# Four stages of attention and convolution on one core: a lap later for the values, a ring of three, scaled unit matrices for the inverses, ones in the first laps

## The reference

```python
x = _L0_conv_ref(x, ...)   # non-local block: theta, phi, g (64 channels), phi and g pooled 2x2 to M0 = 256
                           # softmax over the 256 pooled pixels, product with g, W, batch norm, + x
x = _L1_conv_ref(x, ...)   # wavelet block
x = _L2_conv_ref(x, ...)   # one head:  alpha = softmax(q^T k), out = v alpha^T, projection, + x
x = _L3_conv_ref(x, ...)   # eight heads of 16 channels: attn = softmax(q^T k * temp), out = v attn^T
                           # projection, + x, group norm, MLP, + x
```

## Time and profile before

| | |
|---|---|
| median of three runs | 1834.67 us (1830.48 to 1840.71) |
| the profiled execution | 1839.56 us, span 1838.0 us, mean granted TensorE clock 0.874 |
| PE | 1558.0 us busy (85%) |
| DVE | 1125.7 us (61%) |
| ACT | 816.3 us (44%) |
| POOL | 274.4 us (15%) |

### The profile page before, as it was taken

The page is one execution under the profiler, slowest core; times in us unless marked ns, Lnnn a source line. Parts: engine busy times, 40 slices in busy tenths (PEclk is TensorE's granted clock), DMA queues, the critical chain, the costliest instruction groups (busy, mean ns, idle before and its releaser), DMA issues.

```text
span 1838.0 us, 20837 instructions
## 1 busy us (share of the span) xinstructions
PE 1558.0 (85%) x6468; PEld 690.1 (38%) x6468; DVE 1125.7 (61%) x1912; ACT 816.3 (44%) x1514; POOL 274.4 (15%) x305
## 2 busy tenths in 40 slices
PE   6579769998889889899889898899889888986992
PEld 3236325433343335333353334333343335322430
DVE  5454564766568584877558574777567573766601
ACT  1113301465327552465327552466326562763770
POOL 5003012110130103110130102200140104010000
PEclk6779957998889899898889898998888899987995
DMA  2000022012120303011120303002020303022101
GB/s 51 12 12 7 6 35 47 12 20 50 22 45 7 81 1 64 8 29 53 19 49 7 81 1 59 14 18 64 12 54 7 69 3 64 7 69 43 29 12 36
DMA packets 31569, 58.64 MB, mean 32 GB/s; under 512 B 14678, under 2 KB 16862, under 8 KB 31456
## 3 DMA queue, kind: packets, MB, share of 16 engines
q1 hardware_dynamic: 27296, 50.41, 12.8%
q0 software_dynamic: 4160, 6.83, 2.5%
HBM read 14.37 MB, written 4.50 MB: 10 GB/s over the span
## 4 chain that ended last, share of the span: by engine, by line
PE 64%; DVE 15%; issue 9%; ACT 4%; DMA 3%; SPq 3%; POOL 2%; DVEq 0%; ACTq 0%; POOLq 0%
PE ps L1337 64%; DVE mx L1283 5%; DVE x L1189 3%; ACT p L1015 2%; DVE x L1232 1%; SPq L689 1%; DMA invw<-inverse_sums 1%; DMA qp<-q3h 1%; POOL kp L838 1%; DVE mx L1279 1%; DVE x L1237 1%; DVE x L1196 1%; DVE hn L1226 1%; DVE x L1195 1%; SPq L666 1%
## 5 line engine op out<-in xcount | busy, mean ns | idle before, releaser
L1283 DVE TENSOR_REDUCE mx<-ps 128x1 f32<-128x512 f32 x1024 | 647.9, 683 | 267.5 <-PE ps L1337 265.6
L1015 ACT ACTIVATE p<-ps 128x512 f32<-128x512 f32 x1024 | 551.4, 599 | 313.7 <-PE ps L1337 312.6
L1337 PE MATMUL ps<-kp,qp 63*128 63x512 f32 x1024 | 417.1, 508 | 69.7 <-DVE mx L1283 34.1
L1337 PE MATMUL ps<-qp,kp 64*128 64x512 f32 x1024 | 382.1, 468 | 17.1 <-ACT p L1015 12.4
L1337 PEld LDWEIGHTS ps<-qp,kp 64*128 64x128 f32 x1024 | 165.6, 192 | 359.0 <-ACT p L1015 283.4
L1337 PE MATMUL ps<-p,vt 128*32 128x512 f32 x2048 | 295.6, 633 | 3.8 <-ACT p L1015 2.4
L1337 PEld LDWEIGHTS ps<-kp,qp 63*128 63x128 f32 x1024 | 176.1, 203 | 192.6 <-DVE mx L1283 124.0
L980 ACT ACTIVATE p<-ps 128x512 f32<-128x512 f32 x128 | 76.3, 597 | 255.8 <-PE ps L1337 231.1
L1337 PE MATMUL ps<-p,vT 128*128 128x512 f32 x256 | 143.5, 662 | 2.5 <-ACT p L980 2.4
L849 POOL TENSOR_TENSOR acc<-acc,p 128x512 f32<-128x512 f32 x96 | 126.2, 1315 | 63.4 <-ACT p L980 60.3
L1279 DVE TENSOR_REDUCE mx<-ps 128x1 f32<-128x512 f32 x128 | 82.1, 682 | 37.2 <-PE ps L1337 37.2
(11 more groups left out here) (192 smaller groups left out, 1663.5 us busy)
## 6 DMA issues: line engine op xcount, KB each, us to landing
qp<-q3h SPq DMA_DIRECT2D x128, 64.0 KB, 2.9
xin<-in_x SPq DMA_DIRECT2D x8, 512.0 KB, 4.6
acc<-inverse_sums SPq DMA_DIRECT2D x16, 256.0 KB, 3.4
kp<-k3h POOLq DMA_DIRECT2D x64, 64.0 KB, 4.1
qp<-q3l SPq DMA_DIRECT2D x64, 64.0 KB, 3.2
x3a<-x SPq DMA_DIRECT2D x8, 512.0 KB, 4.6
kp<-k3h SPq DMA_DIRECT2D x64, 64.0 KB, 2.5
x3b<-x3a SPq DMA_DIRECT2D x8, 512.0 KB, 2.9
```

Source lines behind the costliest of these rows:

```text
L1015: a.activation(p3[:, s % 2, i, :], ps[:, SB + (u + 1) % 3, :], ACT.Exp).then_inc(sem("p3_ready"), 1)
L1283: v.tensor_reduce(mx3[:, i, c, h:h + 1], ps[:, bank, :], AX.X, ALU.max).then_inc(sem("mx3_ready"), 1)
L1337: return nc.tensor.matmul(o, l, r, start=start, stop=stop)
```

## The change

Four things are changed together.

1. The values product of the eight-head attention moves from the third to the fourth lap of the next step (`i == 3`). `p3` becomes a ring of three steps, taken by `step % RING` over both groups; the wait before a step's exponentials is for the values product of three steps before. The buffer `p2` of the one-head attention is now the third slot of that ring, so the first exponential of the one-head attention waits for the values product that read this slot last, and the third step's exponentials wait for all values and sums of the one-head attention.
2. The inverses of the first block. Eight products take 128 pixels of `x1` each as the weights and 64 columns of ones, so that the sums of 128 pixels lie on 128 partitions; DVE takes one reciprocal of 128x8 into `inv0`, and multiplies the unit matrix `ident` with four columns of it at a time, which makes four diagonal blocks in a half of `x1`; PE multiplies ones with that half, which puts the inverse of each pixel on all partitions, and ACT copies it to `x1`. The steps behind are numbered two higher.
3. `fill` in the first window puts four `keep_clock` products behind each of laps 0 to 17, where two stood in all.
4. The semaphores `v_ones` and `k_ones` become one, `heads_set`, and those who asked for either ask for all five writes.

Cut to its core (the tables of `STEADY` and `LAST` change in the same way as `FIRST`: products in steps 27, 29, 31, 33 and 35, ACT's copies in 30 and 32; in `STEADY` 29 and 31 are both in lap 155):

```diff
+RING = 3
-    "fill": "000000000110000000000000000000000000000000000000010000...
+    "fill": "444444444444444444000000000000000000000000000000010000...
-            "L0": {...27: 152, 29: 155, 31: 156, 33: 161},
+            "L0": {...27: 152, 29: 155, 31: 155, 33: 156, 35: 161},
...
-        p2 = sb("p2", [128, 4, HALF])
-        p3 = sb("p3", [128, 2, GH, HALF])
+        p3 = sb("p3", [128, RING, GH, HALF])
+        p2 = p3[:, RING - 1, :, :]
...
+                for h in range(NH):
+                    yield at(bt, "L0", 30 + 2 * h)
+                    wait(act, sem("inv0_ps"), bt, NH + 1, h + 2)
+                    a.copy(half(x1, h), ps[:, bank_of(bt), :]).then_inc(sem("inv0_ready"), 1)
...
+                elif u == 0:
+                    wait(act, sem("pv3_done"), bt + -2, NG * STEPS, NG * STEPS - 2)
...
-                            if i == 0 and step >= 2:
-                                wait(act, sem("pv3_done"), bt, NG * STEPS, step - 1)
+                            if i == 0 and step >= RING:
+                                wait(act, sem("pv3_done"), bt, NG * STEPS, step - RING + 1)
+                            elif i == 0 and step == RING - 1 and attention:
+                                wait(act, sem("pv2_done"), bt + 1, A2_TILES)
+                                wait(act, sem("acc_steps"), bt + 1, (NC - 1) * NH)
...
-                            a.activation(p3[:, s % 2, i, :], ps[:, SB + (u + 1) % 3, :], ACT.Exp).then_inc(sem("p3_ready"), 1)
+                            a.activation(p3[:, step % RING, i, :], ps[:, SB + (u + 1) % 3, :], ACT.Exp).then_inc(sem("p3_ready"), 1)
...
-                for h in range(NH):
-                    yield at(bt, "L0", 28 + 2 * h)
-                    wait(dve, sem("den0_ps"), bt, NH, h + 1)
-                    v.reciprocal(half(x1, h), ps[:, bank_of(bt), :]).then_inc(sem("inv0_ready"), 1)
+                yield at(bt, "L0", 28)
+                wait(dve, sem("inv0_ps"), bt, NH + 1, 1)
+                link(v.reciprocal(inv0[:], ps[:, bank_of(bt), 0::CI]))
+                for h in range(NH):
+                    v.tensor_tensor(half(x1, h).rearrange("p (c q) -> p c q", q=128), ident[:].unsqueeze(1).to_broadcast([128, NC // 2, 128]),
+                                    inv0[:, NC // 2 * h:NC // 2 * (h + 1)].unsqueeze(2).to_broadcast([128, NC // 2, 128]), ALU.mult).then_inc(sem("diag0_ready"), 1)
...
+                yield at(bt, "L0", 27)
+                wait(pe, sem("p0_added"), bt)
+                for c in range(NC):
+                    last = mm(ps[:, bank_of(bt), CI * c:CI * (c + 1)], part(x1, c), ones[:, 0:CI])
+                last.then_inc(sem("inv0_ps"), 1)
+                for h in range(NH):
+                    yield at(bt, "L0", 29 + 2 * h)
+                    wait(pe, sem("diag0_ready"), bt, NH, h + 1)
                     if h:
                         wait(pe, sem("inv0_ready"), bt, NH, h)
-                    else:
-                        wait(pe, sem("p0_added"), bt)
-                    mm(ps[:, bank_of(bt), :], ones[:], half(x1, h)).then_inc(sem("den0_ps"), 1)
+                    mm(ps[:, bank_of(bt), :], ones[:], half(x1, h)).then_inc(sem("inv0_ps"), 1)
...
-                        if heads and 0 <= q < HEAD_LAPS and i == 2 and s:
+                        if heads and 0 <= q < HEAD_LAPS and i == 3 and s:
...
-                                last = mm(ps[32 * k:32 * (k + 1), VB, :], vt3[g][:, j, k, :], p3[:, (s - 1) % 2, k, :],
+                                last = mm(ps[32 * k:32 * (k + 1), VB, :], vt3[g][:, j, k, :], p3[:, (g * STEPS + s - 1) % RING, k, :],
```

More of the change, by code:

```diff
@@ L520, in build @@
         x1 = sb("x1", [128, N])
+        inv0 = sb("inv0", [128, NC])
         fused = sb("fused", [128, Q])
@@ L706, in passes @@
                             if mb.is_number(0):
-                                sp.wait_ge(sem("k_ones"), 3)
+                                sp.wait_ge(sem("heads_set"), 5)
                             sp.dma_start(raw(nmrow[0:1, :]).rearrange("p (a b) -> p a b", b=128), raw(nm2T[:])).then_inc(sem("nm2_row_in"), 16)
@@ L834, in pack @@
                     if bt.is_number(0):
-                        pool_e.wait_ge(sem("k_ones"), 3)
+                        pool_e.wait_ge(sem("heads_set"), 5)
                     carry_wait(bt, g)
@@ L1007, in passes @@
                             step = g * STEPS + s
-                            if i == 0 and step >= 2:
-                                wait(act, sem("pv3_done"), bt, NG * STEPS, step - 1)
+                            if i == 0 and step >= RING:
[3 more added lines that the diff above has]
+                                wait(act, sem("acc_steps"), bt + 1, (NC - 1) * NH)
                             elif i == 0:
-                                wait(act, sem("pv3_done"), bt + -1, NG * STEPS, NG * STEPS - 1 + step)
+                                wait(act, sem("pv3_done"), bt + -1, NG * STEPS, min(NG * STEPS, NG * STEPS - 1 + step))
                             u = g * TILES + q
                             wait(act, sem("s3_ps"), bt, NG * TILES, u + 1)
-                            a.activation(p3[:, s % 2, i, :], ps[:, SB + (u + 1) % 3, :], ACT.Exp).then_inc(sem("p3_ready"), 1)
+                            a.activation(p3[:, step % RING, i, :], ps[:, SB + (u + 1) % 3, :], ACT.Exp).then_inc(sem("p3_ready"), 1)
                         if i == 3 and s and s % NC == 0:
@@ L1106, in late_start @@
                 for t in vt3:
-                    v.memset(t[:], 1.0).then_inc(sem("v_ones"), 1)
-                v.memset(raw(qp[:]), 0.0).then_inc(sem("k_ones"), 1)
-                v.memset(raw(nmrow[:]), 0.0).then_inc(sem("k_ones"), 1)
-                v.memset(raw(kp[:]), 1.0).then_inc(sem("k_ones"), 1)
+                    v.memset(t[:], 1.0).then_inc(sem("heads_set"), 1)
+                v.memset(raw(qp[:]), 0.0).then_inc(sem("heads_set"), 1)
+                v.memset(raw(nmrow[:]), 0.0).then_inc(sem("heads_set"), 1)
+                v.memset(raw(kp[:]), 1.0).then_inc(sem("heads_set"), 1)
             def linker(stage, bt, per):
@@ L1167, in non_local @@
             def non_local(bt):
-                link = linker("l0", bt, 2)
+                link = linker("l0", bt, 3)
                 for h in range(NH):
@@ L1185, in non_local @@
                                     ALU.max, negate=True).then_inc(sem("nm0_ready"), 1)
+                yield at(bt, "L0", 28)
+                wait(dve, sem("inv0_ps"), bt, NH + 1, 1)
+                link(v.reciprocal(inv0[:], ps[:, bank_of(bt), 0::CI]))
                 for h in range(NH):
[L1187 to L1189 removed]
+                    v.tensor_tensor(half(x1, h).rearrange("p (c q) -> p c q", q=128), ident[:].unsqueeze(1).to_broadcast([128, NC // 2, 128]),
+                                    inv0[:, NC // 2 * h:NC // 2 * (h + 1)].unsqueeze(2).to_broadcast([128, NC // 2, 128]), ALU.mult).then_inc(sem("diag0_ready"), 1)
                 for h in range(NH):
[L1191 removed]
+                    yield at(bt, "L0", 34 + 2 * h)
                     wait(dve, sem("y0_ps"), bt, NH, h + 1)
@@ L1442, in non_local @@
                     mm(ps[:, bank_of(bt), :], part(ph, k // NH), half(th, k % NH)).then_inc(sem("s0_ps"), 1)
+                yield at(bt, "L0", 27)
[3 more added lines that the diff above has]
+                last.then_inc(sem("inv0_ps"), 1)
                 for h in range(NH):
-                    yield at(bt, "L0", 27 + 2 * h)
+                    yield at(bt, "L0", 29 + 2 * h)
+                    wait(pe, sem("diag0_ready"), bt, NH, h + 1)
                     if h:
                         wait(pe, sem("inv0_ready"), bt, NH, h)
-                    else:
-                        wait(pe, sem("p0_added"), bt)
-                    mm(ps[:, bank_of(bt), :], ones[:], half(x1, h)).then_inc(sem("den0_ps"), 1)
+                    mm(ps[:, bank_of(bt), :], ones[:], half(x1, h)).then_inc(sem("inv0_ps"), 1)
                 for h in range(NH):
-                    yield at(bt, "L0", 31 + 2 * h)
+                    yield at(bt, "L0", 33 + 2 * h)
                     if h:
@@ L1610, in passes @@
                 if bt.is_number(0):
-                    pe.wait_ge(sem("v_ones"), 2)
+                    pe.wait_ge(sem("heads_set"), 5)
                     pe.wait_ge(sem("wo_in"), 16)
-                    pe.wait_ge(sem("k_ones"), 3)
+                    pe.wait_ge(sem("heads_set"), 5)
                 heads, attention = bt.exists(), (bt + 1).exists()
```

1 line of the change is left out of this document (removed), and 32 rows, old and new, of tables (FIRST, LAST, STEADY).

## The result

The changed kernel takes 1850.16 us (median of 19 runs, 1841.84 to 1866.84) against 1836.56 us (19 runs, 1829.01 to 1847.69) before: a ratio of 1.0076, 95% interval 1.0052 to 1.0100. It is slower by 14 us, where 40 us less were forecast.

A forecast was written before the change was run, and what follows sets the result against it. PE, 85% busy, idled 39.0 us for the first layer's reciprocal and 14.8 us for exponentials. Saving 26 + 8 + 2.5 + 3 = 39.5 us takes the profiled 1839.56 us to 1800 us, as a median 1795 us, range 1779 to 1817 us.

The forecast's parts named there:

- Values one lap later: Main loop: values product in the fourth lap cuts PE's waits for exponentials; 3 us less, between 14.8 gain and 9.4 loss.
- Denominators, five windows: Ends of windows 0 to 4: small products and a 128x8 reciprocal save 5.2 us each at full clock, 26 us.
- second and third image: First window: shorter waits for these images' last reciprocals and shorter pairs with `wg`; 2.5 us less, at most 5.9.
- the first rival: New denominator chains: the clock falls all the same, so only 16 us are gained, 1819 us; chance 0.12.
- First image: Start of first window: fillers keep the clock up and the new denominators are shorter; 8 us less (6 to 10).
- the fourth: Rival for the whole kernel: PE is the bound, so added fillers and small products cost their length, 1880 us; chance 0.03.
- The third: Rival at window ends: next window's maxima wait for DMA-brought `qp` rows, five windows gain nothing, 1827 us; chance 0.04.
- The sum: Whole kernel: 26 + 8 + 2.5 + 3 = 39.5 us less, forecast 1795 us; chance 0.76.

The follow-up runs named there:

- run 2: Kernel before with the values part alone: values product in the fourth lap, ring of three shared with p2; ratio to before 1.0216.
- run 9: Changed kernel with norm steps one lap later and the next image's first maxima tile moved from lap 92 to 93 in steady windows; 1805.11 us.
- run 1: Changed kernel with the values product back in the third lap, all else kept; 1802.36 us, ratio to before 0.9824.
- run 4: Changed kernel with the norm steps ahead of the eight heads one lap later in the steady windows; 1841.80 us, ratio to before 1.0033.
- run 5: Kernel before with the denominators part alone (small products, 128x8 reciprocal, scaled unit matrices, ACT's copies, joined semaphore); ratio to before 0.9873.
- run 7: Kernel before with denominators part and fillers, values product in the third lap, ring of two; ratio to before 0.9867.
- run 8: run 1's kernel with more first-window fillers: two behind each of laps 18 to 56, one behind each of laps 161 to 220; 1847.83 us.
- run 10: run 1's kernel with two fillers behind each of laps 18 to 56; 1804.66 us, ratio to before 0.9830.
- run 12: run 1's kernel with laps 92 to 95 holding 0, 0, 3, 2 maxima tiles in place of 1, 0, 3, 1; 1809.86 us.
- run 6: Kernel before with the fillers alone, four behind each of the first 18 laps; ratio to before 0.9993, 1.3 us less.

## Why the prediction was wrong

- **Values one lap later, -3 us (14.8 us of gain to 9.4 us of loss): this step failed.** Measured alone it is +40 us (32 to 47 by run 2's interval). Its first half came true and was worth little: in the trace of before the values product starts within 0.15 us of its fourth exponential in 63 of 256 steps, afterwards in 2; the third lap's score tile then starts so in 62, as was said. What the step left out was the other side of the move. I asked who waits for the values product and for how long, and priced that; I did not ask what the product had been lying beside. It stood in PE's order ahead of one more score tile and one more maxima tile, and the second of these waits for DVE or for a DMA at two places of every window. The Trainium skill (PSUM — Partial Sum Buffer, "Engine vs sequencer instructions") says that matmuls start in program order; the rows agree, since the product whose operands were there (the fourth exponential ended at 612.93 us) stands behind the tile that waits until 619.83 us. Two moves of steps, with the product left in the fourth lap, took back 45 of the 48 us (1850.2 to 1805.1 us), and PE's waits at the two places went with them, so these two places are shown to carry most of the loss. One reservation: neither move was run as it stands with the product in the third lap, and they may gain something by themselves (the second groups of run 9 are 5.7 us shorter than run 1's). The first groups keep 10.0 us of the loss in the table (412.6 against 402.6 us), 1.0 to 1.5 us in each window, which no run took apart.
- **Denominators, five windows, -26 us: held in mechanism and nearly in size; second and third image, -2.5 us: not shown.** Alone they gave 23 us (13 to 33) for the 28.5 us. By the traces the five ends gave 18.0 us in the changed kernel and 27.1 us in run 1. Images two and three gained nothing in the changed kernel: from the first product of the denominators to the end of the pair with `wg` they take 15.29 and 14.58 us, where they took 14.52 and 12.69 us, and the granted clock there is 0.67 and 0.53, where it was 0.76 and 0.73. At the windows' ends eight small products took 2.00 us at full clock (2.3 us by the row). The estimate from the formula of the Trainium skill (TensorE: Matmul & The Clock Gate, "LDWEIGHTS (loading the stationary operand)") was 1.7 us. DVE's part was covered by the values product and the maxima, as worked out. What kept the changed kernel at 18.0 us was the first rival, the low clock: it came in three windows of five there and in one of five in run 1. I had given it 0.12 for all five together. I had taken full clock because the longest idle stretch would be 0.65 us and 0.69 us had gone with the full rate; the stretches came out at 0.68 to 0.77 us, and the clock behind them was at either level. The move of the values product seems to have a part in it: with the new denominators the ends of windows 0 to 4 ran long in 3, 3 and 4 of five windows where the product stands in the fourth lap (the changed kernel, runs 4 and 9), and in 1, 1, 2, 0, 0 and 0 where it stands in the third (runs 1, 5, 7, 8, 10 and 12). How it would do so is open.
- **First image, -8 us: nearly right in the trace, not seen in the medians.** In the trace the pair starts 5.2 us earlier (forecast 6.3) and ends 6.8 us earlier (forecast 7.8). The stretch behind POOL's sum ran at the lower clock, as I had said of its start, but I had priced the small products at 2.3 us even there (3.67 us) and the pair was right (1.92 us). In the medians the fillers give 1.3 us (between 6.6 less and 4.0 more), while the trace of run 6 has a lead of 5.7 us up to the first pair of window 0. Whether it is lost later or only lies within the measurement is open.
- **The rivals.** The time came out on the side of the fourth, slower, to which I gave 0.03, but not by its mechanism: PE's busy time rose by 29.6 us, and run 6 shows that the fillers cost nothing. The third, that the next window doesn't follow because of rows of `qp` that DMAs bring, named the right wait in the wrong place: it is in the middle of the window, at the first maxima tile.
- **The sum.** With the values step at nothing the working gives 1798 us, and run 1, which leaves it out, has 1802 us. That they lie so near is in part luck: in the traces of run 1 and of before the window ends gave 27.1 us for the 26, the first window gave 2.9 us for the 10.5 of the three images, and the groups of four heads, for which this sum has nothing, gave 4.4 + 6.0 us.

## What to carry to other kernels

When a piece of work moves along an engine's order, price it twice: what it waits for in its new place, and what waits it was covering in the old one. To find the second, look in the trace for the stretches in which the other engines or DMAs are busy with something that this engine will need next, and see whether the moved piece runs there. A change of several parts is worth splitting before it is judged: here a gain of 23 us and a loss of 40 us stood in one edit.

## What was not expected of the hardware

- A short wait went with far more than its own length. 16.1 us less of waiting at one place came with 37 us; over the 20 us behind it the granted clock was 0.63 after a wait of 2.11 us, and 0.83 after one of 0.66 us. The Trainium skill (TensorE: Matmul & The Clock Gate, "HAM oscillation") has a kernel whose waits for DMAs lowered the clock each time. These rows do not show that: the clock was at 0.50 in the 4 us ahead of the wait already, and with the longer wait it came back later.
- Products put in to raise the clock did so in the first image (0.50 before and 1.00 after from 20 to 40 us), and did not between 240 and 320 us, where PE is busy for 20.00 of each 20 us at 0.50. There each of the sixty cost some 0.65 us of the program's time (the 34.9 us, and 4.1 us that the other fillers had saved by 234 us).
- The window's end ran at either clock with the same idle times: PE stood for 0.77 us ahead of the second product of ones in window 1 at full speed, and for 0.68 us in window 2 at 0.62. In window 2 the granted clock had been 1.00 over the 14 us up to 884 us, with one idle stretch of 0.77 us, as in window 1, and fell then. The idle times there do not settle the level by themselves, and what does is open.
